# Two graph layers on one core: first gathers from columns of their own, four pairs from x, zeros and loads moved in the prologue

## The chip, the cores and the metric

The kernel runs on one core of one Trainium2 chip. The metric is the device time of a whole execution in microseconds (us). The profile shows one further execution: its span runs from the first to the last instruction, and the engines are named as the profile names them: PE (TensorE; PEld is its weight load), DVE (VectorE), ACT (ScalarE), POOL (GpSimd) and SP (SyncE, which here only issues DMAs). A q behind an engine's name (SPq) is its sequencer.

## The reference

There are 6250 nodes with 128 features, and 100,000 edges that arrive sorted by their target `dst`. The first layer sends a message along each edge and sums at the target, the second sums neighbours; each ends in a layer norm.

```python
# layer 0
msg_input = jnp.concatenate([h[src], h[dst], edge_feat], axis=-1)
messages = jax.nn.silu(msg_input @ W1 + b1) @ W2 + b2
agg = jax.ops.segment_sum(messages, dst, num_segments=h.shape[0])
h_new = jax.nn.silu(jnp.concatenate([h, agg], axis=-1) @ W3 + b3) @ W4 + b4
x = _layernorm(x + h_new + h)
# layer 1
z = (1.0 + eps) * h + jax.ops.segment_sum(h[src], dst, num_segments=h.shape[0])
z = jax.nn.relu(z @ W1 + b1) @ W2 + b2
x = _layernorm(x + relu(layernorm(z + h) * gamma + beta))
```

## The kernel before

**Tiling.** The edges are cut into 196 groups of 512 (`GE`), a group being 4 columns (`CH`) of 128 edges; two groups are a pair, and the first layer goes through the 98 pairs one by one. The nodes are 49 tiles of 128, loaded as 12 blocks of 4 tiles and a last block of one.

**Prologue.** SP loads the blocks of x into `x_rows` (which is the memory of `T`), and among them the sources (`src_rows`, behind block 5) and the targets (`dst_rows`, behind block 8). `blocks(...)` writes out a loop over the blocks for each engine, whose stages lag by whole blocks, with single bodies put in at a block by `only_at`. For a block PE transposes x (L1152), ACT keeps the transpose (L973; for blocks 0 to 7 in the slots of `gath`), PE multiplies it with the first part of W1 (L1160), and DVE adds b1 (`keep_A`, L1545) and writes a tidy copy to `xT` (L1552; for blocks 8 to 11 ACT does so at the end, L979). SP stores the result to the table `src_term` in HBM (`store_A`, L688 and L691). So that table holds, for every node, its term as a source. Beside this the source and target rows are turned into columns: DVE makes floats of them (`to_float`), PE transposes (`turn_rows`), DVE copies to `src_col` or `dst_col` (`cols_of`); and the least targets of the groups give each pair the base of its window of nodes (`least_dst`, `diagonals`, `spread_bases`, `window_bases`, `relative_dst`). POOL sets constants and then makes `terms_r` of the edge weights, 4 instructions (L866).

**Gathers.** POOL then issues every gather of the first layer (`gather_sources`, L873): an indirect DMA for each column, 4 for a group, 8 for a pair, in order, without interruption by other work until the last pairs. The indices of pair 0 and on are columns of `src_col`. A gather goes to one of 8 slots of `gath` (`RING`), group g to slot g mod 8, and has to wait until PE has used what group g - 8 left there (the semaphore `pre_ps`). The first `FROM_X` = 2 pairs are gathered from x itself, since the table is not stored yet; the first gather from the table waits for all stores of it (`source_table_stored`). What comes from x is transposed by PE a step later (`turn_from_x`, L1211), copied by DVE (`keep_from_x`, L1661) and multiplied by the weights in the pair's sum (`add_from_x`, L1219 and L1221), in the place of one matmul with the identity (L1240).

**Steps of the first layer.** `steps(...)` writes out a software pipeline for each engine. In step s SP loads the targets and edge features of pair s (`load_pair`, L715 and L729); ACT takes the window of x (`window_x`); and with lag 1 PE turns the edge features of pair s - 1 (`turn_ef`, L1201, L1203), DVE compares targets (`windows`, L1923), ACT copies (`edge_features`, L1013, L1014). With lag 2 PE makes the sum before the activation of pair s - 2 (`pre_sums`: L1233 and L1240, which raise `pre_ps`), ACT the Silu (L1022), DVE the one-hots (L1649). With lag 3 PE sums the messages of pair s - 3 (`message_sums`, L1250, L1252), and DVE adds them into `S` and the degrees into the first row of `T` (`add_sums`, L1934, L1935, L1938). On each engine the bodies of a step follow one another in the order in which they are listed, and an engine does nothing out of order. Into the steps are put, on DVE, the pieces of a sort of the edges that the second layer needs (`sort_edges`: at step 4 `make_keys`, L1702 to L1707, at steps 5 to 16 three exchanges each, L1736 to L1744), and once the products of weights (`weight_products`): at step 4 PE transposes w2 (L1189), waits for DVE's copy (L1637, at DVE's step 5), multiplies (L1191, L1192), and waits for DVE's second copy (L1639, L1640). The four quarters of `S`, and of the first row of `T`, are zeroed by ACT at steps 0 to 3 (`zero_part`, L993, L994), the first after all stores of the table.

**The end.** When all pairs are summed, the first layer's output is in HBM, and the second layer runs: its gathers, one-hots and matmuls, PE busy in nearly all of it. It begins only behind the last output of the first layer.

The order of the diff's two places in the steps is set by these lines of before:

```python
steps(pe, ..., of_pair(1, turn_ef), of_pair(2, pre_sums), ..., of_pair(3, message_sums),
      at_steps({4: weight_products, **{k + 1: lambda k=k: turn_from_x(k) for k in range(FROM_X)}}), ...)
steps(dve, ..., at_steps({5: weight_products, **{k + 2: lambda k=k: keep_from_x(k) for k in range(FROM_X)}}),
      ..., of_pair(1, windows), of_pair(2, one_hots(...)), of_pair(3, add_sums), (0, NPAIR, sort_edges), ...)
```

## Time and profile before

| | us |
|---|---|
| runs of before | 1882.76, 1891.93, 1894.49 |
| median of them | 1891.93 |
| the profiled execution: its span | 1500.6 |
| median of the runs less that span | 391.3 |

For the profiled execution the profile gives its span alone and no whole time of its own, so its own whole time stands here as that span and 391.3 us around it, which makes it the median run. The runs of before lie 0.6% apart.

The page of the profile counts an engine's busy time as a share of the span; the chain that ended last is followed back from the last instruction. In a timeline a row is: start (us from the span's start), duration in us, engine, line, operation, what it writes <- what it reads, shapes, count, and in brackets the idle time before it with what ended it. Neighbouring instructions that are alike make one row.

### The profile page before, as it was taken

Reading aid. Unit: us, or ns where it says so; the run is one execution under the profiler, and the core shown is the slowest. Engines: PE = TensorE matmul, PEld = TensorE weight load, DVE = VectorE, ACT = ScalarE, POOL = GpSimd, SP = SyncE. Lnnn points to the kernel's source line nnn. Section 1 sums busy time; section 2 is a strip of 40 time slices with the busy share of each in tenths; the row PEclk is TensorE's granted clock in tenths of the full one; section 3 lists DMA queues with packets and bytes.
Section 4 is the critical chain, followed back from the end, with each engine's and each line's share of the span. In section 5 each row is a group of like instructions: output and inputs, shape, how many; then the busy total and the mean of one; then the engine's idle time right before and its main releaser. Section 6 shows DMA issues by size and latency. Waiting matters only on the chain.

```text
span 1500.6 us, 31339 instructions
## 1 busy us (share of the span) xinstructions
PE 1285.9 (86%) x8165; PEld 1063.6 (71%) x8165; DVE 1014.5 (68%) x2310; ACT 642.1 (43%) x1257; POOL 1107.0 (74%) x1164
## 2 busy tenths in 40 slices
PE   6788789778777889888888888885999999999992
PEld 6666667556556667767767776764899999998982
DVE  4678888677665565665566656643666888878866
ACT  2744556555555555555556555551111111111111
POOL 5777777777777777777777777777777777777771
PEclk9898889999998999999999999997999999999996
DMA  6533333333336454454455445433887778778731
GB/s 206 135 85 92 93 95 94 95 96 91 95 90 119 118 138 125 126 136 131 125 131 133 125 128 135 113 80 105 258 261 230 208 230 241 222 230 241 213 92 47
DMA packets 189124, 214.15 MB, mean 143 GB/s; under 512 B 60426, under 2 KB 149517, under 8 KB 189011
## 3 DMA queue, kind: packets, MB, share of 16 engines
q1 hardware_dynamic: 138399, 131.62, 28.9%
q0 software_dynamic: 36352, 74.52, 21.3%
q10 hardware_dynamic: 14260, 6.68, 1.6%
q8 instruction: 49, 0.80, 0.2%
q14 instruction: 64, 0.52, 0.1%
HBM read 202.74 MB, written 9.85 MB: 142 GB/s over the span
## 4 chain that ended last, share of the span: by engine, by line
POOL 42%; PE 32%; issue 15%; DVE 4%; DMA 4%; SPq 1%; ACT 1%; DVEq 0%; ACTq 0%; POOLq 0%
POOL gath L873 42%; PE bank L1434 9%; PE bank L1410 8%; PE bank L1362 4%; DMA gath<-src_term,src_col 2%; PE bank L1240 2%; PE bank L1250 2%; PE bank L1233 2%; PE bank L1421 1%; DMA T<-in_x 1%; DMA gath<-layer_input,src_col 1%; PE bank L1396 1%; PE bank L1383 1%; PE bank L1441 0%; PE bank L1456 0%
## 5 line engine op out<-in xcount | busy, mean ns | idle before, releaser
L873 POOL DMA_INDIRECT gath<-src_term,src_col x768 | 737.2, 960 | 234.2 <-issue 230.2
L873 POOL DMA_INDIRECT gath<-layer_input,src_col x336 | 329.6, 981 | 105.6 <-issue 100.6
L1240 PE MATMUL bank<-gath,ident 128*128 128x512 f32 x384 | 218.3, 652 | 114.5 <-DMA gath<-src_term,src_col 113.8
L1233 PEld LDWEIGHTS bank<-terms_r,terms_l 128*128 128x128 f32 x1568 | 209.4, 201 | 83.1 <-issue 69.2
L1233 PE MATMUL bank<-terms_r,terms_l 128*128 128x128 f32 x1568 | 219.6, 286 | 30.4 <-ACT msg L1022 22.0
L1923 DVE TENSOR_SCALAR_CACHE_REDUCE terms_l<-dst_bc,node_col 64x512 f32<-64x512 int32 x196 | 221.0, 1128 | 13.1 <-issue 7.2
L1250 PEld LDWEIGHTS bank<-oh,msg 128*128 128x128 f32 x1568 | 198.7, 202 | 26.9 <-issue 26.1
L1934 DVE TENSOR_TENSOR S<-S,bank 128x128 f32 x98 | 28.1, 286 | 270.2 <-PE bank L1252 178.2
L1250 PE MATMUL bank<-oh,msg 128*128 128x128 f32 x1568 | 202.3, 285 | 0.0
L1434 PE MATMUL bank<-S 128*128 128x288 f32 x672 | 170.0, 406 | 0.1
L1649 DVE TENSOR_TENSOR oh<-bank,dst_rel 128x1024 f32<-128x1024 f32 x140 | 169.8, 1213 | 0.0
L1240 PEld LDWEIGHTS bank<-gath,ident 128*128 128x128 f32 x384 | 61.2, 201 | 129.7 <-DMA gath<-src_term,src_col 129.4
L1434 PEld LDWEIGHTS bank<-S 128*128 128x128 f32 x672 | 124.5, 190 | 31.1 <-issue 0.2
L1022 ACT ACTIVATE msg<-bank 128x512 f32<-128x512 f32 x196 | 115.8, 599 | 59.8 <-PE bank L1240 57.4
L1013 ACT COPY terms_l<-bank 64x512 f32<-64x512 f32 x196 | 113.7, 580 | 40.0 <-PE bank L1203 28.6
L1076 ACT COPY S<-bank 128x512 f32<-128x512 f32 x84 | 49.2, 586 | 185.8 <-PE bank L1410 181.8
L1993 DVE TENSOR_TENSOR S<-bank,dst_of 128x2304 f32<-128x2304 f32 x44 | 112.0, 2548 | 10.1 <-PE bank L1434 3.8
L1014 ACT COPY terms_r<-bank 64x512 f32<-64x512 f32 x196 | 113.4, 578 | 0.0
L1035 ACT ACT_TABLE_LOAD x48 | 61.6, 1283 | 66.9 <-DVE mv L2025 66.4
L1362 PE MATMUL bank<-oh,gath 128*128 128x128 f32 x672 | 84.4, 279 | 5.1 <-DMA gath<-layer_input,src_col 5.1
L1362 PEld LDWEIGHTS bank<-oh,gath 128*128 128x128 f32 x672 | 80.4, 195 | 5.7 <-DMA gath<-layer_input,src_col 5.7
L1987 DVE TENSOR_SCALAR xT<-xT,even_odd 128x1024 f32<-128x1024 f32 x84 | 60.5, 762 | 5.4 <-DMA xT<-sorted_src 5.4
(219 smaller groups left out, 1754.7 us busy)
## 6 DMA issues: line engine op xcount, KB each, us to landing
dst_bc<-in_dst SPq DMA_DIRECT2D x195, 128.0 KB
...
```

What stands on the lines that cost most here:

```text
L873: g.indirect_dma_start(out=to[:, j * D:(j + 1) * D], out_offset=None, in_=table[0:rows, :], in_offset=bass.IndirectOffsetOnAxis(ap=indices ...
L1013: a.copy(terms_l[r, u, h, :, :], bank[4][r, 0:P].unsqueeze(1).to_broadcast([W, CH, P]))
L1014: last = a.copy(terms_r[r, u, 1 - h, :, :], bank[4][r, P:2 * P].unsqueeze(1).to_broadcast([W, CH, P]))
L1022: a.activation(msg[:, 2 * (m % 2) + h, :], bank[h][:, :], ACT.Silu).then_inc(msg_made, 1)
L1233: mm(bank[h][:, j * D:(j + 1) * D], terms_l[:, u, h, j, :], terms_r[:, u, h, j, :], start=j == 0, stop=False)
L1240: mm(bank[h][:, :], ident[:, :], gath[:, slot, :], start=False, stop=True).then_inc(pre_ps, 1)
L1250: mm(bank[2 + u][:, 0:PW], msg[:, 2 * u + c // CH, c % CH * D:(c % CH + 1) * D], oh[:, u, c, :], start=c == 0, stop=c == 2 * CH - 1)
L1362: last = mm(bank[2 + u][:, 0:PW], gath[:, s, c % CH * D:(c % CH + 1) * D], oh[:, u, c, :], start=c == 0, stop=c == 2 * CH - 1)
L1410: last = mm(bank[h][:, c * D:(c + 1) * D], src_hot[:, u, w, e], x_near[m][h * CH + c][:, w, :], start=w == 0, stop=w == 1)
L1434: last = mm(bank[4][:, 0:DW], rows_kept[:, c // CH, c % CH * D:(c % CH + 1) * D], dst_hot[:, u, c, :], start=o % LATE == 0 and c == 0, sto ...
L1649: ve_.tensor_tensor(oh[:, u, :, :], iota_ps.unsqueeze(1).to_broadcast(shape), dst_rel[:, ds((k + first) * (2 * CH), 2 * CH)].unsqueeze(2). ...
L1923: ve_.tensor_scalar(terms_l[r, u, h, :, :], dst_bc[r, u, :].rearrange("n (p j) -> n j p", j=CH), node_col[r, ds(k, 1)], None, ALU.is_equal ...
```

## The change

- The sources of the first 8 groups are loaded straight as columns into `first_src`, by a DMA ahead of all others on SP, and POOL waits for that load alone before its first gather.
- `FROM_X` goes from 2 to 4: four pairs are gathered from x. The two more have room of their own (`from_x_more`), and the transposed copies go back to where the rows came from instead of into `gath`. The gathers of groups 8 to 15 wait for a turn (`from_x_turned`) instead of `pre_ps`. `weight_products` moves with `FROM_X`: PE's half to step 5, DVE's to step 6.
- `dst` rows are loaded first, behind block 5, `src` rows behind block 8; the work on each moves along in DVE's and PE's prologue. The semaphores of both become shared counts (`rows_prep`, `rows_turned`, `cols_ready`).
- `S` is zeroed by ACT in the prologue at blocks 1, 2, 4 and 8. The first row of `T` is zeroed by one DMA from the first row of `S` (`zero_degrees`), which SP issues at step 0 once all stores of the table have landed. ACT also makes `terms_r` (16 activations at block 8) and writes `xT` for block b - 1 at block b.
- The load of pair 0 is issued behind the table's store 8, ahead of the last four stores.

```diff
-FROM_X = 2
+FROM_X = 4
...
+        first_src = sb("first_src", [P, 2 * FROM_X, CH], I32)
+        from_x_more = sb("from_x_more", [P, 2 * FROM_X - 4, CH * D])
...
+            sp.dma_start(first_src[:, :, :], src[0:2 * FROM_X * GE].rearrange("(g p j) -> p g j", p=P, j=CH)) \
+                .then_inc(first_src_in, 16)
             for blocks_of, to_in in zip(X_BLOCKS, x_in):
                 for b in blocks_of:
                     load_block(b, to_in)
                     if b == 5:
+                        load_rows(sp, dst_rows, dst, dst_in)
+                    elif b == 8:
                         load_rows(sp, src_rows, src, src_in)
-                    elif b == 8:
-                        load_rows(sp, dst_rows, dst, dst_in)
-            for b in range(NB + 1):
-                store_A(b)
...
-            sp.wait_ge(consts, 1)
-            steps(sp, NPAIR - 2, (1, SORTED, SORTED + 1, SORTED + 2), of_unit(9, load_unit0), of_pair(0, load_pair),
-                  at_steps({1: load_weights, SORTED: store_chunks, SORTED + 1: load_bases,
+            def later_pair(k, m, q):
+
+                if not (isinstance(k, int) and k == 0):
+                    load_pair(k, m, q)
+
+            def zero_degrees():
+
+                for u in range(4):
+                    sp.wait_ge(A_out[u], 16 * A_BLOCKS[u])
+                sp.wait_ge(zeroed, STEPS)
+                sp.dma_start(T[0:1, :], S[0:1, :]).then_inc(degrees_zeroed, 16)
+
+            for b in range(NB + 1):
+                if b == NB - 3:
+                    load_pair(0, 0, 0)
+                store_A(b)
+            steps(sp, NPAIR - 2, (1, SORTED, SORTED + 1, SORTED + 2), of_unit(9, load_unit0), of_pair(0, later_pair),
+                  at_steps({0: zero_degrees, 1: load_weights, SORTED: store_chunks, SORTED + 1: load_bases,
                             SORTED + 2: early_rows_stored}), of_early(0, load_early))
             either_order(sp, ordered1, any_order)
...
+                if k == 0:
+                    pool.wait_ge(first_src_in, 16)
                 if k == FROM_X:
+                    pool.wait_ge(cols_ready, OF_SRC)
                     source_table_stored()
                 for g in (2 * k, 2 * k + 1):
                     if k < FROM_X:
-                        gather_rows(x, N, g, src_col[:, g * CH:(g + 1) * CH], gathered[g], from_x[g])
+                        gather_rows(x, N, g, first_src[:, g, :], gathered[g], from_x[g])
                         continue
-                    if g >= RING:
+                    if g >= 2 * FROM_X + RING:
                         pool.wait_ge(pre_ps, done(g - RING))
+                    else:
+                        pool.wait_ge(from_x_turned, g - RING + 1)
                     gather_rows(A_d, N, g % RING, src_col[:, g * CH:(g + 1) * CH], gathered[g % RING])
...
-            pool.wait_ge(src_ready, 1)
             skewed(NPAIR + BRIDGED, [(0, gather_sources), (9, rsqrt0_of)])
...
-            blocks((0, keep_x))
+            def edge_weights(u, h):
+
+                if u == 0 and h == 0:
+                    act.wait_ge(own_rows_made, 1)
+                    act.wait_ge(wef_in, 16)
+                for j in range(CH):
+                    c = h * CH + j
+                    last = a.activation(terms_r[:, u, h, j, :], wef[:, :], ACT.Copy, scale=own_rows[:, c:c + 1])
+                last.then_inc(wef_ready, 1)
+
+            def order_last_xT(b, u, t, nt):
+
+                if RING <= b < NB:
+                    act.wait_ge(x_kept_made, done(b))
+                    a.copy(xT[:, cols(b, BT)].rearrange("d (p t) -> d p t", t=BT),
+                           x_kept[b].rearrange("d (t p) -> d p t", t=BT)).then_inc(last_xT_made, 1)
+
+            def zero_part(s):
+
+                quarter = slice(s * NPAD // STEPS, (s + 1) * NPAD // STEPS)
+                n = NPAD // STEPS // 2
+                if s == 0:
+                    act.wait_ge(consts, 1)
+                a.copy(S[:, quarter].rearrange("p (h n) -> p h n", h=2),
+                       xt[:, 1, 0:1].unsqueeze(2).to_broadcast([P, 2, n])).then_inc(zeroed, 1)
+
+            def while_blocks_come():
+
+                zero_part(3)
+                for u in range(2):
+                    for h in range(2):
+                        edge_weights(u, h)
+
+            blocks((0, keep_x), (1, order_last_xT), (0, only_at({
+                1: lambda: zero_part(0), 2: lambda: zero_part(1), 4: lambda: zero_part(2), 8: while_blocks_come})))
             act.wait_ge(wef_ready, 4)
-            act.wait_ge(x_kept_made, done(NB))
-            for b in range(RING, NB):
-                a.copy(xT[:, cols(b, BT)].rearrange("d (p t) -> d p t", t=BT),
-                       x_kept[b].rearrange("d (t p) -> d p t", t=BT)).then_inc(last_xT_made, 1)
             act.wait_ge(xT_made, done(RING - 1))
             act.wait_ge(last_xT_made, NB - RING)
             act.wait_ge(base_ready, 1)
-
-            def zero_part(s):
-
-                quarter = slice(s * NPAD // STEPS, (s + 1) * NPAD // STEPS)
-                n = NPAD // STEPS // 2
-                zeros = xt[:, 1, 0:1].unsqueeze(2)
-                if s == 0:
-                    for u in range(4):
-                        act.wait_ge(A_out[u], 16 * A_BLOCKS[u])
-                a.copy(S[:, quarter].rearrange("p (h n) -> p h n", h=2), zeros.to_broadcast([P, 2, n]))
-                a.copy(T[0:1, quarter].rearrange("p (h n) -> p h n", h=2),
-                       zeros[0:1].to_broadcast([1, 2, n])).then_inc(zeroed, 1)
...
-            steps(act, NPAIR - 2, range(STEPS), at_steps({s: lambda s=s: zero_part(s) for s in range(STEPS)}),
-                  of_unit(8, hidden0), of_unit(10, store0), of_unit(11, start_T),
+            steps(act, NPAIR - 2, (), of_unit(8, hidden0), of_unit(10, store0), of_unit(11, start_T),
...
-                6: lambda: turn_rows(src_rows_f, src_prep, None, src_turned), 10: spread_bases})))
-            turn_rows(dst_rows_f, dst_prep, src_ready, dst_turned)
+                6: lambda: turn_rows(dst_rows_f, OF_DST), 7: spread_bases,
+                10: lambda: turn_rows(src_rows_f, OF_SRC)})))
             pe.wait_ge(A_made, done(NB))
-            pe.wait_ge(dst_ready, 1)
+            pe.wait_ge(cols_ready, 2)
...
-                  at_steps({4: weight_products, **{k + 1: lambda k=k: turn_from_x(k) for k in range(FROM_X)}}),
+                  at_steps({FROM_X + 1: weight_products, **{k + 1: lambda k=k: turn_from_x(k) for k in range(FROM_X)}}),
...
-                4: lambda: to_float(src_rows, src_rows_f, src_in, src_prep),
-                6: lambda: cols_of(src_turned, src_col, P).then_inc(src_ready, 1),
-                7: lambda: to_float(dst_rows, dst_rows_f, dst_in, dst_prep), 8: least_dst, 9: diagonals,
-                11: window_bases})))
-            cols_of(dst_turned, dst_col, LAST_P).then_inc(dst_ready, 1)
-            relative_dst()
-
-            dve.wait_ge(src_ready, 1)
...
-                    ve_.tensor_copy(gath[:, g, :], bank[5 + h][:, :]).then_inc(from_x_kept, 1)
+                    ve_.tensor_copy(from_x[g], bank[5 + h][:, :]).then_inc(from_x_kept, 1)
...
-                dve.wait_ge(zeroed, STEPS)
+                dve.wait_ge(degrees_zeroed, 16)
...
-                5: weight_products, **{k + 2: lambda k=k: keep_from_x(k) for k in range(FROM_X)}}), *in_banks(9, rows0),
+                FROM_X + 2: weight_products, **{k + 2: lambda k=k: keep_from_x(k) for k in range(FROM_X)}}), *in_banks(9, rows0),
```

**SP, from the last stores of the table to the load of pair 2.** First the rows of before: all stores, then the loads of pairs 0 and 1 (L715, L729), then the weights (L742).

```order
L688 DMA src_term<-T 128x512 [waits A_made] x12
L691 DMA src_term<-T 128x128 [waits A_made]
L715 DMA dst_bc<-in_dst 64x512 [waits ohT_made,consts]
L715 DMA dst_bc<-in_dst 64x512
L729 DMA ef_s<-in_edge_attr 128x2x64 [waits ef_turned]
L715 DMA dst_bc<-in_dst 64x512 [waits ohT_made]
...
L742 DMA w<-in_L_gnn_W 128x128
```

The same place in the changed kernel, where L692 and L695 are the stores, L719 and L733 the loads of a pair, L840 the zeroing of the degrees and L746 the weights:

```order
L692 DMA src_term<-T 128x512 [waits A_made] x9
L719 DMA dst_bc<-in_dst 64x512 [waits ohT_made]
L719 DMA dst_bc<-in_dst 64x512
L733 DMA ef_s<-in_edge_attr 128x2x64 [waits ef_turned]
L692 DMA src_term<-T 128x512 [waits A_made] x3
L695 DMA src_term<-T 128x128 [waits A_made]
L840 DMA T<-S 1x16x392 [waits x1_in1,x1_in0,zeroed,A_out1,A_out0]
L719 DMA dst_bc<-in_dst 64x512 [waits ohT_made]
...
L733 DMA ef_s<-in_edge_attr 128x2x64 [waits ef_turned]
L746 DMA w<-in_L_gnn_W 128x128
```

Pair 0's load has moved ahead of four stores, and pair 1's load now stands behind a DMA that waits for every store to have landed (`A_out0`, `A_out1`, `x1_in0`, `x1_in1`).

**DVE, around the weight products.** Of before: the add of pair 1, `make_keys` (L1702 to L1707), the weight products (L1635 to L1640), then the windows of pair 4, the one-hots of pair 3, the add of pair 2, and only then the first exchange of the sort (L1736).

```order
L1938 TENSOR_TENSOR T<-T,bank 1x64
L1702 TENSOR_SCALAR dst_rows_f<-dst_rows_f,row_min 112x512 [waits sort_steps]
...
L1635 TENSOR_SCALAR one_eps<-one_eps 128x1 [waits w_in]
L1637 COPY w2t<-bank 128x128 [waits w2_turned]
L1639 COPY w<-bank 128x128 [waits w23_ps]
...
L1923 TENSOR_SCALAR terms_l,deg_col<-dst_bc,node_col 64x512 [waits sums_ps,pre_ps,dst_bc_in0]
...
L1649 TENSOR_TENSOR oh<-bank,dst_rel 128x1024 [waits sums_ps]
...
L1736 COPY bank<-src_rows_f 112x256 [waits sort_steps]
```

Of the changed kernel (L1967 is the end of an add, L1731 `make_keys`, L1690 the copy of what came from x, L1952 windows, L1678 one-hots, L1765 to L1773 exchanges, L1664 to L1668 the weight products):

```order
L1731 TENSOR_SCALAR dst_rows_f<-dst_rows_f,row_min 112x512 [waits sort_steps]
...
L1690 COPY from_x_more<-bank 128x512 [waits from_x_turned] x2
L1952 TENSOR_SCALAR terms_l,deg_col<-dst_bc,node_col 64x512 [waits sums_ps,pre_ps,dst_bc_in0]
...
L1678 TENSOR_TENSOR oh<-bank,dst_rel 128x1024 [waits sums_ps]
...
L1967 TENSOR_TENSOR T<-T,bank 1x64
L1765 COPY bank<-src_rows_f 112x256 [waits sort_steps]
L1769 TENSOR_TENSOR src_rows_f<-src_rows_f,bank 112x128x2 [waits sort_steps]
...
L1773 TENSOR_TENSOR src_rows_f<-src_rows_f,bank 112x64x2x2 [waits sort_steps]
L1664 TENSOR_SCALAR one_eps<-one_eps 128x1 [waits w_in]
L1666 COPY w2t<-bank 128x128 [waits w2_turned]
L1668 COPY w<-bank 128x128 [waits w23_ps]
```

The weight products stood directly behind `make_keys`; now they stand one step later, behind the first three exchanges of the sort.

**PE, the end of step 5 and the start of step 6 in the changed kernel** (L1281 and L1283 are the message sums of pair 2, L1220 to L1223 the weight products, L1232 the edge features of pair 5, L1264 and L1271 the sum of pair 4, which raises `pre_ps` for group 8):

```order
L1281 MATMUL bank<-oh,msg 128x128 [waits msg_made,sums_added,oh_made]
...
L1283 MATMUL bank<-ident,deg_col 1x128
L1220 MATMUL bank<-ident,w 128x128 [waits w_in]
L1222 MATMUL bank<-w,w2t 128x128 [waits w2_ready]
L1223 MATMUL bank<-w,b_col 1x128
L1232 MATMUL bank<-ident,ef_s 128x128 [waits efT_made,ef_in1,w23_ready]
...
L1264 MATMUL bank<-terms_r,terms_l 128x128 [waits msg_made,ohT_made,efT_made]
...
L1271 MATMUL bank<-gath,ident 128x512 [waits gathered_0]
```

In before the same weight products stood between steps 4 and 5, ahead of the sum of pair 3; they now stand between steps 5 and 6, ahead of the sum of pair 4.

## Rows read from the trace of the kernel before

**Rows 1.** The page: the span, and the chain that ended last, by engine.

```profile
span 1500.6 us, 31339 instructions
...
POOL 42%; PE 32%; issue 15%; DVE 4%; DMA 4%; SPq 1%; ACT 1%; DVEq 0%; ACTq 0%; POOLq 0%
```

**Rows 2.** POOL's waits up to 1060 us: waited for, us in total, times, longest.

```profile
POOL gath L873 <- issue: 239.4, 785, 0.3
...
POOL gath L873 <- PE bank L1240: 4.0, 13, 0.3
```

**Rows 3.** Timeline of POOL: pair 0, pair 8, pair 16, the last gather of the layer.

```profile
22.49 1.15 POOL L873 DMA_INDIRECT xs<-in_x,src_col  x1 [5.89 <-DVE src_col L1536]
...
103.88 0.96 POOL L873 DMA_INDIRECT gath<-src_term,src_col  x1 [0.30 <-issue]
...
185.18 0.95 POOL L873 DMA_INDIRECT gath<-src_term,src_col  x1 [0.31 <-issue]
...
1033.73 0.96 POOL L873 DMA_INDIRECT gath<-layer_input,bridge_rows  x1 [0.30 <-issue]
```

**Rows 4.** Timeline of PE: the last x blocks arrive, first ends of step 1.

```profile
4.14 1.94 PE L1152 MATMUL bank<-ident,T 128*128 128x128 f32 x8 [4.14 <-DMA T<-in_x]
...
28.06 1.12 PE L1152 MATMUL bank<-ident,T 128*128 128x128 f32 x4 [4.63 <-DMA T<-in_x]
...
44.05 0.45 PE L1201 MATMUL bank<-ident,ef_s 128*128 128x128 f32 x1 [6.31 <-DMA ef_s<-in_edge_attr]
```

**Rows 5.** Timelines of DVE, ACT and SP: end of the table's making, its landing, pair loads.

```profile
36.14 0.41 DVE L1574 COPY base_bc<-bank 128x256 f32<-128x256 f32 x1
...
37.99 0.87 DVE L1545 TENSOR_TENSOR T<-bank,b_bc 128x512 f32<-128x512 f32 x2
...
41.73 1.50 ACT L993 COPY S<-xt 128x1568 f32<-128x1568 f32 x1 [1.64 <-DMA src_term<-T]
...
39.05 0.43 SPq L691 DMA_DIRECT2D src_term<-T  x1
...
40.84 0.59 SPq L729 DMA_DIRECT2D ef_s<-in_edge_attr  x1
...
42.63 0.59 SPq L729 DMA_DIRECT2D ef_s<-in_edge_attr  x1
```

**Rows 6.** Timeline of PE: starts of steps 2 to 5, first sum of step 5.

```profile
49.89 0.45 PE L1201 MATMUL bank<-ident,ef_s 128*128 128x128 f32 x1 [2.42 <-ACT terms_r L1014]
...
57.87 1.04 PE L1211 MATMUL bank<-ident,xTs 128*128 128x128 f32 x8
58.74 0.27 PE L1201 MATMUL bank<-ident,ef_s 128*128 128x128 f32 x1
...
66.62 0.33 PE L1201 MATMUL bank<-ident,ef_s 128*128 128x128 f32 x1
...
77.77 0.48 PE L1201 MATMUL bank<-ident,ef_s 128*128 128x128 f32 x1 [0.57 <-DVE cdeg L1640]
...
80.17 1.78 PE L1240 MATMUL bank<-gath,ident 128*128 128x512 f32 x2
```

**Rows 7.** Timeline of DVE: copies of turned rows, weights, add of pair 2, next windows.

```profile
58.51 1.29 DVE L1661 COPY gath<-bank 128x512 f32<-128x512 f32 x2 [3.66 <-PE bank L1211]
...
75.56 0.28 DVE L1637 COPY w2t<-bank 128x128 f32<-128x128 f32 x1
...
85.99 0.29 DVE L1934 TENSOR_TENSOR S<-S,bank 128x128 f32 x1 [4.80 <-PE bank L1252]
...
90.78 1.13 DVE L1923 TENSOR_SCALAR_CACHE_REDUCE terms_l<-dst_bc,node_col 64x512 f32<-64x512 int32 x1
```

**Rows 8.** Timeline of PE: the sum of pair 12, first group.

```profile
163.69 1.91 PE L1240 MATMUL bank<-gath,ident 128*128 128x512 f32 x2
```

**Rows 9.** DMA queues: packets, MB, share of 16 engines; stretch 20 to 30 us.

```profile
q10 hardware_dynamic: 14260, 6.68, 1.6%
...
20.00:30.00 10.00, 5.37 (x40) 5.18 (x40) 6.56 (x13) 1.76 (x3) 5.98 (x6) 0.85 0.72 256
```

60 lines of the change are left out of this document (29 added, 31 removed).

## The prediction

> **What bounds the kernel now.** I read the chain of waits first, then POOL's waits, then the timelines of the first 100 us. The chain is 42% POOL and 32% PE, with 15% "issue" [rows 1]. The PE part is the second layer, which starts only when the first is done. The POOL part is the row of gathers: it starts at 22.49 us and the last gather ends at 1034.7, which is 1012.2 us for 800 of them [rows 3]. One takes 0.96 us and 0.30 us of issue, so 800 need 1009. The wait list agrees: of the gaps before gathers nearly all are "issue", and only 13 were put down to PE, none above 0.3 us [rows 2]. So POOL never waits in the first layer. A us by which a gather starts earlier is a us off the time, but only while no later gather has to wait. Each gather of group g needs the slot that PE frees with `pre_ps` of group g - 8, four pairs back. That reserve is what has to be counted.
>
> **Start of the gathers.** Before, pair 0 waits for `src_col` until 22.49 [rows 3]. Now it waits for `first_src`. SP issues that at about 0.9 us. The first x block's transposes, which need a load from the same place in the queue, start at 4.14 [rows 4], so I put the first gather at 4.6 and bound it by 4.1 and 9 (twice that). POOL's own constants are no later, and its 4 instructions for the edge weights go to ACT, which idles there while the x blocks come. The start moves by 17.9 us. The 32 gathers from x take 32 x 1.26 = 40.3 us and about 0.6 more for the first ones (the first of before took 1.15 instead of 0.96 [rows 3]), so POOL reaches pair 4, the first that needs the table, at 45.5.
>
> **Is the table there?** The last x blocks come at 28.06 [rows 4] and the last block is ready at 38.86 [rows 5]. The work from one to the other stays, but the window bases (36.14 to 37.99 on DVE [rows 5]) leave that stretch, while the copy of the turned sources enters it, and so does `relative_dst`, which mostly falls into DVE's idle time there. I take 0.5 us off: ready at 38.4. The last store's landing was 2.7 us after its issue (39.05 to 41.73 [rows 5]), so the table is there at 41.3 + d. Here d is the delay of the x loads by what is new on the DMA engines ahead of them: 1024 pieces of 16 bytes, and some 13 more gathers before 28 us. Queue q10 moved 14260 packets of 0.47 KB in 1.6% of 16 engines' span [rows 9], 27 ns each; 1024 on 16 engines would be 64 x 27 ns = 1.7 us. The extra gathers enter a stretch where the engines are busy 72% [rows 9], so half or more of them fits in. I take d = 2 and the bounds 0 and 4. The Trainium skill ("DMA: Bandwidth & Descriptors", section "Bandwidth") has about 10.5 ns for such a packet, an estimate of 0.7 us for the new load; by it d would be 1 and the forecast 1 us lower. No row of before has pieces of 16 bytes. Either way the table is there before 45.5, and pair 4 does not wait.
>
> **The PE chain, which frees the slots.** Without ACT's zeros PE can turn pair 0's features and rows at once, at about 39 + d. Step 2 then needs pair 1's features, and their load now stands behind the zeroing of the degrees, which waits for the whole table: 41.3, one DMA issue 0.5, pair 1's three issues 1.8 (from 41.43, the end of pair 0's, to 43.22 [rows 5]), landing 2.6 us after the issue (as pair 0: 41.43 to 44.05 [rows 4, 5]). Step 2 starts at 46.2 + d; before it was 49.89 [rows 6]. So the removed zeros give 3.7 - d there and no more.
> From there with the steps of before [rows 6]:
> - step 2 lasts 58.74 - 49.89 = 8.85: step 3 at 55.05 + d.
> - step 3 lasts 66.62 - 58.74 = 7.9. Its sum is one of x, as before, but it also gets the turn of pair 2, 0.9 (57.87 to 58.74): step 4 at 63.85 + d.
> - step 4 now holds a sum of x too, so 7.9 + 0.9: step 5 at 72.65 + d. (Before, this step's sum came from the table.)
> - step 5: 7.9, and 1.3 because DVE copies pair 3's turned rows (1.29 [rows 7]) only behind `make_keys`: PE is done with the message sums at 81.85 + d.
> - the weight products. PE transposes w2 and waits for DVE. DVE comes from the add of pair 2, which starts 0.3 later, and runs it and three exchanges first. From that add to the end of the exchanges it was 85.99 to 90.78, 4.8 us [rows 7]; so DVE copies w2 at 87.0 + d. From that copy to PE's next step 75.56 to 77.77, 2.2 [rows 6, 7]: step 6 at 89.2 + d.
> - the sum of pair 4's first group ends 4.2 later, as 77.77 to 80.17 + 1.78 [rows 6], PE being at its lower clock behind such an idle time: 93.4 + d.
>
> With d = 2 this is 95.4. Before, pair 8's first gather started at 103.88 [rows 3]. POOL would be there at 45.5 + 4 x 10.1 = 85.9, and has to wait 9.5 us. Pairs 5, 6 and 7 need only the turns of pairs 1, 2 and 3, at the ends of steps 2, 3 and 4 (57, 66 and 75), and POOL comes at 55.6, 65.7 and 75.8; a us lost there lies within the wait at pair 8. So the gathers move by 103.9 - 95.4 = 8.5 us of the 17.9.
>
> **Behind it.** From step 7 DVE with the sort sets the pace. There the reserve was 185.18 - 165.6 = 19.6 us (pair 12's sum ends at 163.69 + 1.91 [rows 8]; pair 16's gather [rows 3]). DVE's windows of pair 6 come about 5 us later than before by the chain above (step 6's own adds start 2.8 + d later), POOL 8.5 earlier: 19.6 - 13.5 = 6 are left. No wait there. The rest of the first layer has reserves near 30 us, and the second layer is moved as a whole. Other edits (shared semaphores, room for two more pairs, the degrees by DMA instead of 4 copies of ACT) lie beside the gathers and cost nothing; without that cover the DMA's 3 us would still come long before the first add of pair 0.
>
> **Sum.** The execution of the profile stands for the median run, span 1500.6 and 391.3 around it: 1891.9 - 8.5 = 1883.4 us. With d = 0 it is 1881.4, with d = 4 1885.4.
>
> **Rivals.**
> - Nothing stops POOL: pair 8's gather comes at 85.9 instead of 103.9, and 18.0 us arrive in full, 1873.9 us. For it speak the small waits of before [rows 2] and that my PE chain is built of steps run partly at the lower clock. Against it: the sum of pair 4 would have to end at 85.9, 9.5 us before what I worked out, and it has the exchanges and two sums of x ahead of it.
> - The sort's stretch takes the gain back: if DVE came another 6 us later than I have it, the reserve of 19.6 is used up and pair 12 or so waits; with 6 more on top the gain is about 3 us, 1889. For it: DVE is behind its sum there by nearly a whole pair. Against: the chain above already holds the DVE work that is new (4 copies, 2.6 us).
> - Slower: the early gathers take the DMA engines from the x loads. If each of the 13 held them up by its own period of 1.26 us, d would be 16.4, the sum of pair 4 ends at 109.8, and the time is 1891.9 + 5.9 = 1897.8. It decides from d = 10.5 on. For it: between 22.6 and 28.06 PE stands 4.6 us for x blocks [rows 4] while the first gathers of before run. Against: these gathers move 64 KB each, and the engines are not full [rows 9].
> - The change doesn't do what it says: the column load lands late. Up to a first gather near 14 us, pair 8 is still held by PE, and the time stays at 1883.
>
> **How the numbers follow.** The stall at pair 8 has 60%, POOL unhindered 20%, the loss in the sort's stretch 14%, the slower case 6%. The likeliest gives 1883.4 us. The range goes from 1873 (unhindered, a us early) to 1892 (loss in the sort's stretch and the scatter of the median, since single runs of before differ by 12 us). Faster or slower by over 1%, 18.9 us, is about what a measurement of this kernel can tell from no change. Faster by that much: half of the unhindered case and the edge of the others, 16%. Slower by that much: the far part of the slower case, 4%. The rest, 80%, is within 1%.
>
> **What would show it.** In the changed profile: first gather at 4 to 6 us; 32 gathers from x in a row; no wait at pair 4; step 2 on PE near 48; DVE's copy of w2 near 89, behind three exchanges; and one wait of POOL for PE's L1271 of 8 to 10 us, at the gather of pair 8, after which gathers run without a gap and the first layer's last one ends near 1026. I am wrong if that wait is under 3 us, if it stands at pair 4 on the stores, if waits come between pairs 12 and 20, or if x blocks arrive after 34 us.

## The result and the profile after

| | us |
|---|---|
| before, median of 20 runs | 1895.67 (1882.76 to 1908.35) |
| after, median of 20 runs | 1916.06 (1892.99 to 1925.14) |
| ratio after / before | 1.0095, 95% interval 1.0074 to 1.0116 |
| predicted | 1883.4 (1873 to 1892), ratio 0.9955 |

The changed kernel is 0.7 to 1.2% slower. In a second comparison the ratio was 1.0133 (1.0105 to 1.0162). The prediction had the wrong sign.

The page of the kernel after, its span and its chain; [rows 1] of before had 1500.6 us and a chain of 42% POOL:

```profile
span 1918.2 us, 31497 instructions
...
another core or an unknown queue 33%; PE 23%; issue 18%; ACT 9%; DVE 7%; ACTq 3%; DVEq 2%; SPq 1%; DMA 1%; POOLq 0%; POOL 0%
```

"Another core or an unknown queue" and "remote" (below) stand where the profile names no releaser for a wait; the kernel runs on one core, so they tell only that the releaser is not known. The two spans are 418 us apart where the whole times are 20 apart. That puts the trace of before, on which the prediction rests, in doubt; experiment 1 takes it again. POOL's waits up to 1060 us in the kernel after, in the columns of [rows 2]:

```profile
POOL gath L883 <- issue: 165.9, 543, 0.4
POOL gath L883 <- PE bank L1271: 139.5, 35, 14.2
POOL gath L883 <- remote: 83.8, 39, 2.4
POOL gath L883 <- DMA src_term<-T: 27.6, 1, 27.6
POOL gath L883 <- PE bank L1242: 11.5, 3, 4.3
```

POOL waits in nearly every pair. Where the early waits stand is seen in its timeline (as [rows 3]): first gather of pairs 4, 5, 6, 7, 8 and 9.

```profile
71.77 1.52 POOL L883 DMA_INDIRECT gath<-src_term,src_col  x1 [27.59 <-DMA src_term<-T]
84.92 0.95 POOL L883 DMA_INDIRECT gath<-src_term,src_col  x1 [2.89 <-PE bank L1242]
98.90 0.95 POOL L883 DMA_INDIRECT gath<-src_term,src_col  x1 [4.28 <-PE bank L1242]
112.92 0.95 POOL L883 DMA_INDIRECT gath<-src_term,src_col  x1 [4.35 <-PE bank L1242]
136.85 0.95 POOL L883 DMA_INDIRECT gath<-src_term,src_col  x1 [14.23 <-PE bank L1271]
148.48 0.95 POOL L883 DMA_INDIRECT gath<-src_term,src_col  x1 [1.94 <-remote]
```

The 32 gathers from x ended at 44.2, as planned, and then POOL stood 27.6 us for the table. SP issued its last store only at 69.14 (39.05 in [rows 5]; 48.70 in the second trace of before, below). The windows of the prologue say why: between 20 and 40 us nearly nothing runs except the gathers. After, in 10 us each:

```profile
core 0: us, PE busy (x) PEld busy (x) DVE busy (x) ACT busy (x) POOL busy (x), PEclk, DMA share, GB/s
10.00:20.00 10.00, 4.53 (x39) 4.08 (x37) 3.27 (x6) 2.57 (x3) 7.56 (x9) 1.00 0.64 204
20.00:30.00 10.00, 2.90 (x12) 2.53 (x12) 0.00 (x0) 1.98 (x2) 7.56 (x9) 0.56 0.63 197
30.00:40.00 10.00, 0.00 (x0) 0.00 (x0) 1.95 (x4) 0.00 (x0) 7.56 (x9) 0.50 0.41 114
```

The stores, the end of the wait for pair 1's features at the start of step 2, the weight products (DVE's copy of w2 and PE's wait for it), and the start of step 6:

```profile
69.14 0.43 SPq L695 DMA_DIRECT2D src_term<-T  x1
71.06 0.60 SPq L840 DMA_DIRECT2D T<-S  x1
...
76.02 0.47 PE L1232 MATMUL bank<-ident,ef_s 128*128 128x128 f32 x1 [5.59 <-DMA ef_s<-in_edge_attr]
...
130.05 0.28 DVE L1666 COPY w2t<-bank 128x128 f32<-128x128 f32 x1
130.38 0.80 PE L1222 MATMUL bank<-w,w2t 128*128 128x128 f32 x2 [4.99 <-DVE w2t L1666]
132.26 0.48 PE L1232 MATMUL bank<-ident,ef_s 128*128 128x128 f32 x1 [0.57 <-DVE cdeg L1669]
```

### The profile page after: what moved, and what is told of

Same layout as the page of the kernel before. It is cut to its first block, busy times and chain, and to the rows that moved or that the text cites. A ratio compares the mean times of both kernels' runs of the same rounds, so it can differ in the third digit from the quotient of the medians.

```text
span 1918.2 us, 31497 instructions
## 1 busy us (share of the span) xinstructions
PE 1455.3 (76%) x8237; PEld 1167.4 (61%) x8237; DVE 1019.7 (53%) x2314; ACT 631.1 (33%) x1269; POOL 1086.7 (57%) x1160
## 3 DMA queue, kind: packets, MB, share of 16 engines
q0 software_dynamic: 36352, 74.52, 16.0%
## 4 chain that ended last, share of the span: by engine, by line
another core or an unknown queue 33%; PE 23%; issue 18%; ACT 9%; DVE 7%; ACTq 3%; DVEq 2%; SPq 1%; DMA 1%; POOLq 0%; POOL 0%
PE bank L1465 4%; PE bank L1264 4%; PE bank L1271 3%; PE bank L1441 3%; PE bank L1281 2%; ACT msg L1054 2%; DVEq L1958 1%; ACTq L1034 1%; PE bank L1393 1%; DVE oh L1678 1%; DVE terms_l L1952 1%; ACT S L1108 1%; PE bank L1414 1%; ACT L1067 1%
## 5 line engine op out<-in xcount | busy, mean ns | idle before, releaser
L883 POOL DMA_INDIRECT gath<-src_term,src_col x752 | 711.9, 947 | 519.7 <-issue 201.0
L1264 PEld LDWEIGHTS bank<-terms_r,terms_l 128*128 128x128 f32 x1568 | 257.0, 238 | 137.0 <-issue 133.6
L1264 PE MATMUL bank<-terms_r,terms_l 128*128 128x128 f32 x1568 | 272.4, 325 | 63.6 <-issue 50.7
L1281 PE MATMUL bank<-oh,msg 128*128 128x128 f32 x1568 | 221.1, 292 | 78.5 <-issue 50.2
L1281 PEld LDWEIGHTS bank<-oh,msg 128*128 128x128 f32 x1568 | 205.6, 205 | 111.4 <-issue 74.9
L1271 PE MATMUL bank<-gath,ident 128*128 128x512 f32 x376 | 236.4, 710 | 24.5 <-issue 24.2
L1952 DVE TENSOR_SCALAR_CACHE_REDUCE terms_l<-dst_bc,node_col 64x512 f32<-64x512 int32 x196 | 221.9, 1132 | 12.0 <-issue 5.0
L1465 PE MATMUL bank<-S 128*128 128x288 f32 x672 | 192.0, 442 | 30.9 <-ACT S L1108 21.9
L1465 PEld LDWEIGHTS bank<-S 128*128 128x128 f32 x672 | 136.5, 208 | 78.2 <-issue 40.3
L1678 DVE TENSOR_TENSOR oh<-bank,dst_rel 128x1024 f32<-128x1024 f32 x140 | 169.8, 1213 | 0.0
L1393 PE MATMUL bank<-oh,gath 128*128 128x128 f32 x672 | 100.2, 287 | 49.9 <-issue 46.4
L1232 PE MATMUL bank<-ident,ef_s 128*128 128x128 f32 x98 | 34.1, 348 | 95.4 <-issue 48.5
L1271 PEld LDWEIGHTS bank<-gath,ident 128*128 128x128 f32 x376 | 72.1, 233 | 31.7 <-issue 31.5
L1232 PEld LDWEIGHTS bank<-ident,ef_s 128*128 128x128 f32 x98 | 15.1, 155 | 107.8 <-issue 84.2
```

The source lines that it names most:

```text
L883: g.indirect_dma_start(out=to[:, j * D:(j + 1) * D], out_offset=None, in_=table[0:rows, :], in_offset=bass.IndirectOffsetOnAxis(ap=indices ...
L1264: mm(bank[h][:, j * D:(j + 1) * D], terms_l[:, u, h, j, :], terms_r[:, u, h, j, :], start=j == 0, stop=False)
L1271: mm(bank[h][:, :], ident[:, :], gath[:, slot, :], start=False, stop=True).then_inc(pre_ps, 1)
L1281: mm(bank[2 + u][:, 0:PW], msg[:, 2 * u + c // CH, c % CH * D:(c % CH + 1) * D], oh[:, u, c, :], start=c == 0, stop=c == 2 * CH - 1)
L1393: last = mm(bank[2 + u][:, 0:PW], gath[:, s, c % CH * D:(c % CH + 1) * D], oh[:, u, c, :], start=c == 0, stop=c == 2 * CH - 1)
L1465: last = mm(bank[4][:, 0:DW], rows_kept[:, c // CH, c % CH * D:(c % CH + 1) * D], dst_hot[:, u, c, :], start=o % LATE == 0 and c == 0, sto ...
```

## The experiments

"Ratio" is against before on the same chip; a pair's "pace" is the distance of PE's steps 20 to 80, divided by 60; "step n" is from PE's transpose of edge features in step n to that in step n + 1. Experiments 1 to 4 ran on one chip, 5 to 8 on a second, 9 to 12 on a third, 13 to 15 on a fourth. The medians of before were 1896.71, 1945.37, 1941.89 and 1892.89 us there. So only ratios are compared between chips, and the times in us that are expected below are read as ratios to 1897 us.

**1 and 2. Both kernels again** (no edit). Was the trace of before unusual, and is the loss real?

> The kernel before, unchanged, to get a second trace of it. The one trace of before has a span of 1500.6 us, 391 less than its times; the trace of the change has 1918.2, which is its time. Theory A (the first trace was of an unusually quick execution): this one has a span near 1890 us, with gathers of the first layer 11.8 us a pair instead of 10.1, as in the change's trace. Theory B (the trace of before is how before always runs, and the rest lies around the span): span near 1500 us again.

> The change, unchanged, again. Theory A: span near 1915 us, about 20 above r1_before, with the first gather from the table (pair 4) near 70 us because the table lands late. Theory B: span and time as far apart here as in before, so the difference of spans is not that of the times.

Measured: before 1896.54 us (0.9999), after 1920.82 (1.0133). The profiled execution of before took 1908.88 us as a whole, with a span of 1907.0; that of after had a span of 1920.6. The span of before is 406 us more than in [rows 1], and only 2 us lie around it. The first trace was of an execution some 20% quicker than any that was timed. PE's 8165 matmuls were busy for 1285.9 us in it and for 1456.5 us in the second trace, at a mean granted clock of 0.945 and 0.869, so not all of the 406 us are waits. Before as it usually runs, POOL's waits up to 1060 us:

```profile
POOL gath L873 <- PE bank L1240: 125.3, 36, 7.0
POOL gath L873 <- remote: 91.3, 43, 3.2
```

And from POOL's timeline in the same trace the first gathers of pairs 0, 2, 4, 5 and 8:

```profile
24.82 1.21 POOL L873 DMA_INDIRECT xs<-in_x,src_col  x1 [8.92 <-DVE src_col L1536]
...
51.20 0.95 POOL L873 DMA_INDIRECT gath<-src_term,src_col  x1 [5.92 <-DMA src_term<-T]
...
74.54 0.95 POOL L873 DMA_INDIRECT gath<-src_term,src_col  x1 [3.16 <-remote]
...
86.25 0.95 POOL L873 DMA_INDIRECT gath<-src_term,src_col  x1 [1.94 <-remote]
...
121.61 0.95 POOL L873 DMA_INDIRECT gath<-src_term,src_col  x1 [2.10 <-remote]
```

The last store of the table and the starts of steps 2 and 3 in that trace:

```profile
48.70 0.43 SPq L691 DMA_DIRECT2D src_term<-T  x1
...
58.97 0.45 PE L1201 MATMUL bank<-ident,ef_s 128*128 128x128 f32 x1 [2.42 <-issue]
...
77.27 0.27 PE L1201 MATMUL bank<-ident,ef_s 128*128 128x128 f32 x1
```

So before, too, POOL waits at most pairs, 2 to 3 us, and pair 8 is gathered at 121.6 (103.9 in [rows 3]). After it is 136.9 and, in the second trace, 139.6: 15 and 18 us later. From there on the pace is nearly one: 12.8 us a pair before, 12.9 and 12.7 after (the expected 11.8 is in neither). The last gather of the layer ends at 1284.9 before, and at 1300.4 and 1295.4 after. So 15.5 us of delay are left there in one trace of after, 10.5 in the other. Most of what is to be explained lies ahead of pair 8.

**3. Gathers held** (after, with one wait more, so that the prologue runs without gathers beside it):

```diff
                 if k == 0:
                     pool.wait_ge(first_src_in, 16)
+                    pool.wait_ge(A_made, done(6))
```

> The change, with one more wait: the first gather also waits until block 6 of the table is made, near 22 us, which is where before started it. Theory P (the early gathers hold up the prologue: the x loads and what hangs on them): the table lands 15 to 25 us earlier than in r2_after and the time falls back to that of before within 5 us. Theory Q (the loss is made by something else, such as the two more pairs from x or the weight products behind the sort): the time stays within 5 us of r2_after or gets longer.

**4. Two pairs from x** (after):

```diff
-FROM_X = 4
+FROM_X = 2
...
-                    else:
+                    elif g >= RING:
                         pool.wait_ge(from_x_turned, g - RING + 1)
```

> The change with two pairs from x instead of four (and with it the weight products back at step 4 of PE and 5 of DVE); gathers start early all the same but then wait for the table. Theory P: still slower than before by 10 us or more, since 16 gathers run beside the x loads. Theory Q: as quick as before or quicker, ratio 1.00 or under.

Measured: held 1926.14 (ratio 1.0142, 1.0102 to 1.0181), two pairs 1918.26 (1.0121, 1.0071 to 1.017). The held kernel's prologue is whole again; its windows, to be compared with those of after above:

```profile
10.00:20.00 10.00, 7.17 (x51) 6.98 (x50) 6.78 (x13) 5.04 (x6) 0.00 (x0) 0.97 0.60 195
20.00:30.00 10.00, 7.27 (x52) 6.99 (x52) 7.39 (x20) 5.83 (x14) 3.30 (x3) 0.84 0.67 243
30.00:40.00 10.00, 8.12 (x47) 7.44 (x46) 4.30 (x9) 7.31 (x15) 7.56 (x9) 0.67 0.53 150
```

And SP's row of its last store of the table:

```profile
50.80 0.32 SPq L695 DMA_DIRECT2D src_term<-T  x1
```

The table is 20 us earlier, near its place in before (48.70), and the time has not fallen: theory P was right about the table and wrong about the time. The stalled prologue is therefore real, but not by itself the loss. Something takes its place: step 2 lasts 30.7 us here and 27.7 in experiment 4, where before it was 18.3 and in the kernel after 9.4. In that step PE crawls: its matmuls come one by one, with 1 us or more between them.

**5. A pause of POOL's in the kernel before.** Its table gathers are held until pair 0 is summed, so that POOL issues nothing during step 2:

```diff
                 if k == FROM_X:
+                    pool.wait_ge(pre_ps, done(1))
                     source_table_stored()
```

> Before, with one wait more: POOL's gathers of pair 2 and on wait for the two sums of pair 0, so that no gather is issued while PE works on step 2 (77.3 - 59.0 = 18.3 us in the trace of before taken again). Theory G (other engines' instructions and hand-offs come late while POOL issues gathers): step 2 on PE falls to 9 to 12 us, the table gathers start some 15 to 20 us later than 51.2, and the time stays within 5 us of before, 1892 to 1902. Rival T (the early steps are slow whatever POOL does, and the gathers' start sets the time): step 2 still takes 17 to 19 us and the time rises by 10 us or more, to 1907 or over.

Measured: step 2 takes 9.4 us. But the gathers now run beside steps 3 and 4, which take 19.0 and 43.0; pair 8 is at 145.3, and the ratio is 1.0074 (1.0052 to 1.0096). The stretches of step 2, of step 3, and the first 20 us of step 4, in the columns of the windows above:

```profile
57.00:67.00 10.00, 8.81 (x54) 8.68 (x55) 6.09 (x22) 8.67 (x15) 0.00 (x0) 0.65 0.33 84
67.00:87.00 20.00, 11.61 (x78) 9.90 (x76) 4.73 (x7) 6.33 (x10) 15.23 (x16) 0.76 0.25 66
87.00:107.00 20.00, 4.68 (x11) 3.23 (x12) 0.00 (x0) 0.05 (x1) 11.51 (x13) 0.50 0.16 43
```

PE issues 54 matmuls in 10 us while POOL is still, and 11 in the last of these stretches, 20 us long, with POOL gathering for most of it. The gathers begin at 67.19, but PE goes on at its rate for 6 us. The crawl begins only then:

```profile
72.42 1.06 PE L1222 MATMUL bank<-b_bc,ident 128*128 128x128 f32 x8
73.32 0.50 PE L1251 MATMUL bank<-oh,msg 128*128 128x128 f32 x3
74.54 0.38 PE L1251 MATMUL bank<-oh,msg 128*128 128x128 f32 x2 [0.73 <-issue]
75.96 0.39 PE L1251 MATMUL bank<-oh,msg 128*128 128x128 f32 x2 [1.03 <-issue]
```

It is the same beside the first row of table gathers in the second trace of before and in the traces of experiments 4, 7, 8, 9, 10 and 15: the first gap of over 1 us inside a group of matmuls comes 8 to 15 us after the row has begun, and the last one ends by 3.2 us after POOL stops. Why it sets in so late is open. On theory G the half about step 2 came true and the half about the time did not: the pause moved the crawl, and did not remove it. Gathers do have to start in time; rival T's 10 us are nearer than G's.

**6. The weight products back in their place** (after):

```diff
-                  at_steps({FROM_X + 1: weight_products, **{k + 1: lambda k=k: turn_from_x(k) for k in range(FROM_X)}}),
+                  at_steps({**{k + 1: lambda k=k: turn_from_x(k) for k in range(FROM_X)},
+                            FROM_X: lambda: (weight_products(), turn_from_x(FROM_X - 1))}),
...
-                FROM_X + 2: weight_products, **{k + 2: lambda k=k: keep_from_x(k) for k in range(FROM_X)}}), ...
+                **{k + 2: lambda k=k: keep_from_x(k) for k in range(FROM_X)},
+                FROM_X + 1: lambda: (weight_products(), keep_from_x(FROM_X - 1))}), ...
```

> The changed kernel with the weight products back one step (PE's half at step 4, DVE's at step 5, ahead of the first exchanges of the sort); four pairs still come from x. Theory W (their place behind the exchanges costs a good part of the loss): step 6 on PE starts within 13 us of step 5 instead of 19.4, pair 8's gather comes near 132 instead of 139.6, and the time falls from 1921 to about 1911. Rival G (the loss is the late prologue and the slow first steps while POOL gathers): the time stays within 4 us of the changed kernel, 1917 to 1924.

Measured: ratio 1.006 (1.0034 to 1.0087), pair 8 at 134.7, and from step 5 to 6 it is 12.3 us instead of 19.4. The products now lengthen step 4, to 19.4 instead of 13.7. So some 1.4 us of the 7 are won net in these two steps, and pair 8 comes 2 to 5 us earlier than in the two traces of the kernel after. The ratio lies 0.35 and 0.7% under the two of the kernel after, 7 and 14 us, but on other chips, and its interval overlaps that of 1.0095 (1.0074 to 1.0116). Theory W has the direction right; that the products' place cost more than those 2 to 5 us is not shown.

**7. Both undone: held, and two pairs from x** (edits of 3 and 4).

> The changed kernel with two pairs from x and with the gathers held until block 6 of the table is made (near 24 us). What is left of the change: the order of loads, zeros in the prologue, the degrees' DMA, pair 0 loaded ahead of the last stores, pair 1 behind the table. Theory S (early gathers and four pairs from x are the loss, each masking the other when undone alone): the time is that of before within 5 us, 1892 to 1902. Rival R (the rest of the change costs it): 1910 or over, and PE's steps 1 to 3 still take 10 us more than before.

Measured: 1.0042 (1.002 to 1.0064), which is 0.8 and 1.0% below the edits alone. That fits S in that undoing both gives back what neither edit alone did, but 8 us remain, more than S allows, and step 2 is 30.4. PE's timeline in that step shows the crawl:

```profile
57.17 0.48 PE L1233 MATMUL bank<-ident,ef_s 128*128 128x128 f32 x1 [3.84 <-DMA ef_s<-in_edge_attr]
...
66.58 0.27 PE L1253 MATMUL bank<-b_bc,ident 128*128 128x128 f32 x1 [1.46 <-issue]
...
70.81 0.37 PE L1253 MATMUL bank<-b_bc,ident 128*128 128x128 f32 x1 [2.55 <-issue]
72.91 0.37 PE L1253 MATMUL bank<-b_bc,ident 128*128 128x128 f32 x1 [1.73 <-issue]
75.71 0.37 PE L1253 MATMUL bank<-b_bc,ident 128*128 128x128 f32 x1 [2.43 <-issue]
...
82.70 0.37 PE L1243 MATMUL bank<-ident,xTs 128*128 128x128 f32 x1 [2.42 <-issue]
...
87.60 0.42 PE L1233 MATMUL bank<-ident,ef_s 128*128 128x128 f32 x1
```

None of these rows but the first waits for anything that the profile names: inside the crawl the matmuls are of two lines, one after the other, and before each stands 1.4 to 2.6 us of "issue". In the second trace of before the same crawl starts at 67 and ends at 74, where POOL has just stopped for a slot (71.4 to 74.5). Here POOL goes on until 82.4 and the crawl until 85, since groups 8 to 11 no longer wait for a sum, only for a turn.

**8. The first part of the change alone** (before, FROM_X = 2, POOL's edge weights left on POOL):

```diff
+            sp.dma_start(first_src[:, :, :], src[0:2 * FROM_X * GE].rearrange("(g p j) -> p g j", p=P, j=CH)) \
+                .then_inc(first_src_in, 16)
...
+                if k == 0:
+                    pool.wait_ge(first_src_in, 16)
                 if k == FROM_X:
+                    pool.wait_ge(src_ready, 1)
                     source_table_stored()
...
-                        gather_rows(x, N, g, src_col[:, g * CH:(g + 1) * CH], gathered[g], from_x[g])
+                        gather_rows(x, N, g, first_src[:, g, :], gathered[g], from_x[g])
```

> Before, with only the first part of the change: sources of pairs 0 and 1 loaded as columns, and their 16 gathers issued from there, the table gathers waiting for all columns. Theory G: the prologue is held up while these 16 gathers are issued, but ends before the table is due; last store of the table at 48 to 56 us, and the time within 5 us of before, 1892 to 1902. Rival E (any early gather costs as much as the whole change): 1910 or over. Rival T (an earlier start of the gathers moves the end by as much): 1885 or under.

Measured: ratio 0.9965 (0.9943 to 0.9986). First gather at 16.05, last of the 16 at 38.6, last store at 43.71 (48.70 before): the gathers are over when the table is being finished. Pair 8 at 117.3. The time is a little under what theory G gave, and the table came earlier than its 48 to 56; rivals E and T are both out.

**9, 10 and 11. The old wait for a slot put back**, in the kernels of experiments 4, 7 and in the kernel after:

```diff
-                        pool.wait_ge(from_x_turned, g - RING + 1)
+                        pool.wait_ge(pre_ps, done(g - RING))
```

> The changed kernel with two pairs from x, and with the gathers of groups 8 to 11 waiting, as before the change, for the sum of the group eight back instead of for its turn. Theory G2 (PE issues one matmul in 1.4 to 2.8 us for as long as POOL goes on with gathers without a stop; the new wait let POOL go on two pairs longer, which made step 2 28 us instead of 18): step 2 is back at 16 to 20 us, and the time falls from 1.012 to 0.995 to 1.003 of before. Rival D (step 2 is long for another reason: the degrees' DMA, pair 1's late load, the copies' place): step 2 stays at 26 us or more, time 1.008 or over.

> The same wait put back in the kernel of the held gathers with two pairs from x (1.004 of before). G2: step 2 from 30 to 16 to 20 us, time 0.995 to 1.001. Rival D: unchanged, 1.003 or over.

> The changed kernel, four pairs from x, with the gathers of groups 8 to 15 waiting for the sums of groups 0 to 7 instead of for their turns. G2: POOL stops in every one of the steps 2 to 5 and PE isn't slowed there for long; pair 8's gather at 128 to 134 instead of 139.6, time 1.004 to 1.009 of before. Rival (the wait costs what it delays, since the gathers set the time): 1.013 or over.

Measured: 1.0015 (0.9997 to 1.0034), 1.0036 (1.0014 to 1.0058) and 1.0156 (1.0121 to 1.0192). Step 2 is 19.8 and 19.6 in 9 and 10, as G2 says (27.7 and 30.4 without this edit), and pair 8 comes at 124.1 and 123.4. In experiment 9 the time follows: the early gathers of two pairs, ACT's edits, the DMA for the degrees and the moved loads together cost at most 0.34%. In 10 it doesn't, though pair 8 is 8 us earlier; that is a miss. Experiment 11 is a miss too. There POOL stands 39.7 us at pair 4:

```profile
84.05 0.95 POOL L883 DMA_INDIRECT gath<-src_term,src_col  x1 [39.68 <-PE bank L1252]
```

With the prologue already held up (last store of the table at 71.8), the further delay of the gathers is a loss. Between experiments 9 and 11, on one chip, the number of pairs from x differs, and with it the place of the weight products: 1.4% or 26 us for two more pairs.

**12. Plain DMAs for pairs 2 and 3** (before). **13. The same for all 96 pairs of the table** (the condition left out, the rows taken modulo 48 tiles). Both kernels leave out the gather by source, so their results are not those of the reference; they are for their times alone.

```diff
+                    if g < RING:
+                        for j in range(CH):
+                            nc.gpsimd.dma_start(gath[:, g, j * D:(j + 1) * D], A_d[(g * CH + j) * P:(g * CH + j + 1) * P, :]) \
+                                .then_inc(gathered[g % RING], 16)
+                        continue
                     gather_rows(A_d, ...)
```

> Before, with pairs 2 and 3 loaded by plain DMAs of consecutive table rows, 16 issued by POOL in the place of 16 gathers, same bytes and same semaphores; the messages of those two pairs are therefore made from other nodes' rows. Theory G2i (it is POOL's work on gathers that slows PE's issue): step 2 falls from 18 to 9 to 12 us. Rival G2d (it is the traffic or the destination): step 2 stays at 16 or more. The time is not expected to move by more than 0.5%.

> Before, with all 768 table gathers of the first layer replaced by plain DMAs of consecutive table rows issued by POOL, same bytes, slots and semaphores; the first layer's messages are therefore made from other nodes' rows. Theory G2i (POOL's work on gathers slows the hand-offs of the other engines): the first layer's pace falls from 11.9 us a pair to 10 or under, the crawls of PE (gaps of 0.8 us and more inside a group of matmuls) go from some 45 in the first 1050 us to under 15, and the time falls by 10% or more of the first layer, to 0.94 of before or less. Rival G2d (traffic, or the engines' own work, sets the pace): pace 11.5 to 12, time 0.98 or over.

Measured, 12: step 2 is 9.6 us and the ratio 0.9944 (0.9919 to 0.9969). It doesn't decide: the 16 plain DMAs were all issued by 57.3, so POOL was silent in step 2 until 63.16, as in experiment 5. Experiment 13 decides between G2i and G2d: ratio 0.7996 (0.7964 to 0.8029), 1516.18 us, span 1514.1, pace 8.5 us a pair. The gaps of over 0.8 us between two matmuls of one group in the first 1050 us fall from 52 in the second trace of before to 11. From 300 to 900 us, the window of before (second trace):

```profile
300.00:900.00 600.00, 454.29 (x2453) 343.31 (x2451) 300.79 (x711) 264.50 (x525) 367.24 (x384) 0.87 0.35 89
```

and the same window of experiment 13:

```profile
300.00:900.00 600.00, 580.03 (x3793) 464.89 (x3792) 431.69 (x1017) 393.47 (x782) 304.07 (x554) 0.98 0.51 139
```

All engines do half as much again in the same time, PE is busy in 580 of 600 us, and the DMA engines move more (139 GB/s instead of 89). So it is neither the bytes nor the engines' own work that sets the pace of 12.8; what goes with the indirect gathers does. POOL is busy 304 of 600 us in experiment 13 (367 with gathers), so a busy POOL alone does not seem to be enough either.

The first trace of before, with all its gathers, lies near experiment 13 in this window, and it has no gap of that kind at all:

```profile
300.00:900.00 600.00, 510.79 (x3192) 401.41 (x3192) 371.77 (x875) 335.26 (x660) 455.21 (x475) 0.96 0.47 119
```

Its steps 2 to 7 take 8.9, 7.9, 11.1, 8.0, 6.1 and 8.2 us, those of experiment 13 8.6, 7.9, 10.6, 7.7, 6.1 and 8.2, and those of the second trace of before 18.3, 11.4, 16.3, 7.4, 9.0 and 12.9. So the prices that the prediction took from the first trace are those of a PE that gathers do not slow.

**14 and 15. The first part alone once more, and with its gathers still earlier** (POOL's edge weights moved behind the 16 gathers).

```diff
                 if k == FROM_X:
+                    edge_weights()
                     pool.wait_ge(src_ready, 1)
```

> The kernel of the first part alone once more, for a gain that was near the edge of what can be told: 0.994 to 0.999 of before again. If it was chance: 1.0 within 0.002.

> The same, with POOL's four instructions for the edge weights behind the 16 gathers from x, which then start at 4 us instead of 16 and lie beside more of the prologue's work. G2: the prologue is held up by it until about 24 us but has caught up by the last store, which is issued at 44 to 50 us; time 0.997 to 1.002 of before, so not better than the first part alone. Rival (the earlier the better): 0.993 or under.

Measured: 0.9979 (0.9955 to 1.0002) and 1.0012 (0.9985 to 1.0039). Together with experiment 8 the first part alone is a gain of 0.2 to 0.35%, at the edge of what can be told; gathers 12 us earlier (4.0 instead of 15.6) do not add to it. Steps start at 49.5 instead of 48.1.

Pair 8's first gather beside the ratio, for all experiments but 13, whose pace is another:

```
run                      pair 8 at   table's last store   ratio
before (1)                  121.6      48.7               1.000
after (2)                   139.6      71.5               1.013
held (3)                    136.3      50.8               1.014
two pairs (4)               129.8      49.4               1.012
pause in before (5)         145.3      47.9               1.007
products back (6)           134.7      68.9               1.006
held, two pairs (7)         131.2      50.4               1.004
first part (8; 14)    117.3; 116.1  43.7; 43.0            0.997; 0.998
4 with old wait (9)         124.1      50.1               1.002
7 with old wait (10)        123.4      50.6               1.004
after with old wait (11)    141.3      71.8               1.016
plain DMAs, 2 pairs (12)    110.9      46.8               0.994
first part, earlier (15)    117.9      44.8               1.001
```

19 us are 1%. The place of pair 8 gives the sign of each run but the last and in most of them the size to within 8 us; in 3, 4, 5 and 11 it is off by 9 to 15 us, and there is one trace of each kernel for it.

## Why the prediction was wrong

**The execution of the profile.** "The execution of the profile stands for the median run, span 1500.6 and 391.3 around it." This failed first. The span of the second trace is 1907.0, 2 us short of that execution's whole time. The 391 us were not around the span but inside the usual one: the first layer's last gather ends at 1284.9 instead of 1034.7, and the rest is in the second layer. A span 21% short of the median time was there to be seen.

**"POOL never waits in the first layer."** True of that trace alone. In the second it waits 2 to 3 us at most pairs, for PE wherever the profile names a releaser, so a gather that starts earlier gives nothing unless PE is earlier too. The rule that a us at the start is a us off the time fell, and with it the gain of 8.5 us.

**Start of the gathers.** Right: 4.0 against 4.6, and 32 gathers from x in a row to 44.2 against 45.5.

**"Is the table there?"** The step that failed most. I counted only what the gathers take from the x loads (d = 2, bounds 0 to 4). The load of the columns was indeed light, and x blocks were not late: none is waited for after 10 us in the prologue of the kernel after. But PE, ACT and DVE hardly ran beside the gathers (windows above), a cost that the sum put at nothing: ACT stood 22.5 us and DVE 17.0 us at a stretch. The last store was issued at 69.1, and the DMA that waits for all stores at 71.06, where the prediction has 41.3 + d: d was 30, not 2. Against before as it usually runs (last store at 48.70) the table is 20 us late. The threshold of the slower rival was 10.5. That rival had the right sign and the right place, the prologue; its mechanism (DMA engines taken from the x loads) was not the one, and its 1897.8 us too little. The 27 ns for a packet, from another queue's packets, were three times too much (8.5 ns, below), which changed little.

**"The PE chain."** With d = 30 step 2 would start at 76 and step 6 at 119; they came at 76.0 and 132.3. So the wait for pair 1's features, behind the DMA for the degrees, was right. Steps 2 to 5 took 9.4, 13.9, 14.0 and 19.0 us where I had 8.85, 8.8, 8.8 and 16.5 (9.2 and the products' 7.35), 13.4 us more in all. Steps 3 and 4 missed by 5 us each. The extra pairs from x bring 36 matmuls and transposes more for each pair, but the sum had priced them; what it lacked is that PE runs slower beside gathers. In the second trace of before step 3, without any extra pair, took 11.4 us where the first had 7.9. The weight products waited behind three exchanges as worked out: DVE's copy of w2 (L1666) came at 130.05, and PE stood 4.99 us for it. From the add ahead of the exchanges (125.32) to that copy it was 4.7 us, 4.8 predicted. That mechanism was right.

**POOL at pair 8.** One long wait for L1271, of 14.2 us (9.5 predicted), with the place and the engine right; but small ones at pairs 5, 6 and 7 (2.9 to 4.4) that I had excluded, and a wait of 27.6 at pair 4, which was one of the things that would prove me wrong.

**"Behind it."** The reserves of 19.6 and 30 us are not there: pairs from 9 on wait 2 to 3 us each. But before has the same waits in its second trace, and the distance of the kernels does not grow behind pair 8 (15 to 18 us there, 10.5 to 15.5 at the last gather), so nothing more was lost there. The sort's stretch, rival 2, played no part that the traces show.

**What the two errors did together.** By the prediction's own rule pair 8 at 136.9 instead of 103.9 would be a loss of 33 us. The measured one is 20 to 24, since pair 8 of before is usually at 121.6.

**What made the loss**, then, by the runs: (a) 32 gathers without a break beside the prologue stall it until 44 us; with 16 of them it recovers (last store at 49.4 in experiment 4 against 71.5). (b) Two more pairs from x, 26 us on one chip, with (a) and (d) in it; no run has four pairs from x without the one or without the other on that chip, so it is not divided. (c) The wait for a turn instead of a sum lets POOL gather on beside step 2: 1.1% or 20 us where two pairs come from x early (4 against 9, on two chips), nothing that can be told where they are held (7 against 10, on two chips), and no loss where four come from x (11). So in the kernel after itself it is no part of the loss. (d) The weight products a step later: 2 to 5 us by pair 8, 7 to 14 by ratios from different chips. They are not a sum, since each stall hides others. The early gathers of two pairs by the column load are a small gain at most.
